# Scatters that alternate with GpSimd's own copies and sums, in a two-block image kernel on one core

## What is computed

```python
x = x + conv0(ln_c(x))        # shared 1x1 conv and 2 of 4 3x3 expert convs an image, group norm, silu
t = to_tokens(x)              # 16 x 1024 tokens of 128 channels
t = t + ffn0(ln_t(t))         # router takes 2 of 8 experts a token: two gated MLP outputs, weighted and summed
x = from_tokens(t)
x = x + conv1(ln_c(x))        # 3x3 depthwise taps made for each image from its pooled channels
t = to_tokens(x)
t = t + ffn1(ln_t(t))         # router takes 1 of 8 experts a token, up to a capacity
x = from_tokens(t)
```

## Time and profile before

| | |
|---|---|
| median of the timed runs | 2088.33 us |
| the profiled execution, its span | 2373.5 us |
| TensorE busy | 1745.3 us, 74% |
| VectorE busy | 1521.7 us, 64% |
| GpSimd busy | 1040.3 us, 44% |
| ScalarE busy | 1020.1 us, 43% |
| GpSimd: scatters L618 | 384, 387.8 us busy |
| GpSimd: scatters L639 | 448, 471.0 us busy |
| GpSimd: sums L670 and L673 | 32, 75.6 us busy |
| granted TensorE clock, mean | 0.879 |

### The profile page before, as it was taken

The page is one execution under the profiler, slowest core; times in us unless marked ns, Lnnn a source line. Parts: engine busy times, 40 slices in busy tenths (PEclk is TensorE's granted clock), DMA queues, the critical chain, the costliest instruction groups (busy, mean ns, idle before and its releaser), DMA issues.

```text
span 2373.5 us, 40208 instructions
## 1 busy us (share of the span) xinstructions
PE 1745.3 (74%) x8924; PEld 941.9 (40%) x8925; DVE 1521.7 (64%) x5423; ACT 1020.1 (43%) x1718; POOL 1040.3 (44%) x1196
## 2 busy tenths in 40 slices
PE   0387777776667775699999999287877868899822
PEld 0333333333333432354445445154544444444312
DVE  1856555545455554577777777476766647788678
ACT  0433333333233332476666667135455524555411
POOL 0003333333333334576566666525455344666600
PEclk9889888878888887799999999599899979999955
DMA  9300001001000002322222221412211013222044
GB/s 267 102 19 28 28 28 36 28 31 33 33 31 28 27 19 59 87 81 74 71 73 79 74 72 46 106 40 60 72 56 45 18 40 95 72 81 72 19 133 151
DMA packets 180085, 149.22 MB, mean 63 GB/s; under 512 B 19302, under 2 KB 161822, under 8 KB 179960
## 3 DMA queue, kind: packets, MB, share of 16 engines
q1 hardware_dynamic: 153336, 98.05, 14.9%
q0 software_dynamic: 26624, 49.93, 6.2%
HBM read 76.00 MB, written 77.34 MB: 65 GB/s over the span
## 4 chain that ended last, share of the span: by engine, by line
PE 38%; DVE 22%; issue 13%; another core or an unknown queue 11%; ACT 7%; POOL 5%; SPq 2%; DMA 1%; ACTq 1%; DVEq 1%; POOLq 0%
PE banks L734 10%; PE banks L736 9%; PE banks L735 9%; PE banks L729 6%; ACT work L1043 3%; POOL slot_rows L618 2%; SPq L429 2%; DVE small L1896 1%; PE banks L747 1%; PE banks L946 1%; DVE small L1392 1%; DVE small L1247 1%; POOL tokens L673 1%; POOL tokens L670 1%
## 5 line engine op out<-in xcount | busy, mean ns | idle before, releaser
L639 POOL DMA_INDIRECT ffn_rows<-work x448 | 471.0, 1051 | 293.9 <-issue 182.1
L618 POOL DMA_INDIRECT slot_rows<-work,small x384 | 387.8, 1010 | 325.5 <-issue 153.3
L729 PE MATMUL banks<-small,work 128*128 128x128 f32 x1472 | 239.9, 308 | 300.8 <-ACT work L1043 118.2
L729 PEld LDWEIGHTS banks<-small,work 128*128 128x128 f32 x1472 | 193.9, 158 | 379.4 <-issue 170.7
L1784 DVE TENSOR_TENSOR work<-work 128x512 f16<-128x512 f32 x376 | 261.4, 695 | 12.8
L734 PE MATMUL banks<-work,wb_h 128*128 128x512 f16 x648 | 247.7, 382 | 26.6 <-DVE work L1800 9.7
L735 PE MATMUL banks<-work,wb_h 128*128 128x512 f16 x648 | 247.0, 381 | 0.0
L736 PE MATMUL banks<-work,wb_l 128*128 128x512 f16 x648 | 246.9, 381 | 0.0
L734 PE MATMUL banks<-work,wa_h 128*128 128x512 f16 x576 | 243.4, 423 | 3.6 <-ACT work L1074 3.3
L735 PE MATMUL banks<-work,wa_h 128*128 128x512 f16 x576 | 243.1, 422 | 0.0
L736 PE MATMUL banks<-work,wa_l 128*128 128x512 f16 x576 | 241.9, 420 | 0.0
(11 more groups left out here) (307 smaller groups left out, 3110.6 us busy)
## 6 DMA issues: line engine op xcount, KB each, us to landing
wa_l<-slot_rows SPq DMA_DIRECT2D x112, 264.0 KB
work<-ffn_rows SPq DMA_DIRECT2D x48, 512.0 KB, 5.2
ffn_rows<-small SPq DMA_DIRECT2D x32, 256.0 KB, 3.7
work<-in_x SPq DMA_DIRECT2D x16, 512.0 KB, 3.3
out_image<-work SPq DMA_DIRECT2D x16, 512.0 KB, 2.6
ffn_rows<-work POOLq DMA_INDIRECT x448
slot_rows<-work,small POOLq DMA_INDIRECT x384
slot_rows<-small SPq DMA_DIRECT2D x17, 264.0 KB, 4.1
```

The costliest lines, as they stand in the source:

```text
L618: pool_e.indirect_dma_start(slots, bass.IndirectOffsetOnAxis(ap=slot_i[:, row_buffer(p, i, k), tt:tt + 1], axis=0), rows[row_buffer(p, i, ...
L639: pool_e.indirect_dma_start(dst, bass.IndirectOffsetOnAxis(ap=idg[old.v][:, qq, 0:1].bitcast(I32), axis=0), yt[old.u][:, qq, :], None, bou ...
L729: last = pe.transpose(dst[:, tt * P:(tt + 1) * P], x, ident)
```

## The change

In stage A ScalarE's copy of rows[0] to rows[1] is gone. GpSimd makes it in 16 pieces of half a block each (64 floats a partition), between its scatters. The new order is S0(0), copies of block 0; then for each further block t: S0(t), half a copy of block t, a wait for the copies of block t-1, S1(t-1), the other half of block t; at the end S1(7). S0 is a scatter of rows[0], S1 one of rows[1]. `A_rows2_ready` now counts 16 pieces an image. `route_rows` waits in addition until the copies of the image before are done, and VectorE's `route_place` waits for the rows themselves and for the scatters of rows[1] of the image before.

In stage C the two sums of an image are cut into eight quarters, each behind one of the eight scatters of a step. They belong to image i+4 instead of i+3 and come after the borders, with the scatters of image i-2, instead of at the start of the step. The first steps, which have no scatters, make the sums whole, in quarters one after another. `C_added` and `C_half_added` count four an image, and those who wait for them are changed to match.

```diff
--- before.py
+++ after.py
@@ -521,7 +521,7 @@
 
             def load_rows(i):
                 if some(i.b - 1):
-                    sp.wait_ge(sem("C_added"), i.b - 1)
+                    sp.wait_ge(sem("C_added"), (i.b - 1) * 4)
                 for k, dst in ((0, ya), (1, yb)):
                     src = back0[bass.ds(i.b * PIX + k * TOKENS, PIX), :]
                     sp.dma_start(dst[i.u], src.rearrange("(t p) c -> p t c", p=P)).then_inc(sem(f"C_rows_loaded{i.u}"), 16)
@@ -602,7 +602,30 @@
             for x in (*pad_h, *pad_l):
                 pool_e.memset(x, 0.0).then_inc(sem("pads_zeroed"), 1)
 
-            def scatters(p, i, choices):
+            def scatter_row(p, i, k, tt):
+
+                pool_e.indirect_dma_start(
+                    slots, bass.IndirectOffsetOnAxis(ap=slot_i[:, row_buffer(p, i, k), tt:tt + 1], axis=0),
+                    rows[row_buffer(p, i, k)][:, tt, :], None, bounds_check=SLOTS - 1, oob_is_err=False
+                ).then_inc(sem(f"{p}scattered_rows{row_buffer(p, i, k)}"), 16)
+
+            def sum_part(i, k, part):
+
+                n = TPI // 4
+                dst = tokens[:, bass.ds(i.b * TPI + part * n, n), :]
+                src = (ya, yb)[k][i.u][:, part * n:(part + 1) * n, :]
+                if k == 0:
+                    if part == 0:
+                        pool_e.wait_ge(sem(f"C_rows_loaded{i.u}"), i.h * 32 + 32)
+                        apart(pool_e)
+                    pool_e.tensor_tensor(dst, dst, src, ALU.add).then_inc(sem("C_half_added"), 1)
+                else:
+                    if part == 0:
+                        pool_e.wait_ge(sem("C_half_added"), i.b * 4 + 4)
+                        apart(pool_e)
+                    pool_e.tensor_tensor(dst, dst, src, ALU.add).then_inc(sem("C_added"), 1)
+
+            def scatters(p, i, choices, more=None):
 
                 if not live(i, IMAGES):
                     return
@@ -613,12 +636,24 @@
                         pool_e.wait_ge(sem(f"{p}scattered_rows{k}"), 16 * TPI * (IMAGES - 2) * choices // 2)
                         apart(pool_e)
                     pool_e.sem_inc(sem("early_rows"), 1)
-                for k in range(choices):
+                if p == "A_":
                     for tt in range(TPI):
-                        pool_e.indirect_dma_start(
-                            slots, bass.IndirectOffsetOnAxis(ap=slot_i[:, row_buffer(p, i, k), tt:tt + 1], axis=0),
-                            rows[row_buffer(p, i, k)][:, tt, :], None, bounds_check=SLOTS - 1, oob_is_err=False
-                        ).then_inc(sem(f"{p}scattered_rows{row_buffer(p, i, k)}"), 16)
+                        scatter_row(p, i, 0, tt)
+                        for half in range(2):
+                            part = slice(half * (C // 2), (half + 1) * (C // 2))
+                            pool_e.tensor_copy(rows[1][:, tt, part], rows[0][:, tt, part]).then_inc(sem("A_rows2_ready"), 1)
+                            if half == 0 and tt:
+                                pool_e.wait_ge(sem("A_rows2_ready"), i.b * (2 * TPI) + 2 * tt)
+                                apart(pool_e)
+                                scatter_row(p, i, 1, tt - 1)
+                    pool_e.wait_ge(sem("A_rows2_ready"), i.b * (2 * TPI) + 2 * TPI)
+                    apart(pool_e)
+                    scatter_row(p, i, 1, TPI - 1)
+                else:
+                    for tt in range(TPI):
+                        scatter_row(p, i, 0, tt)
+                        if live(more, IMAGES):
+                            sum_part(more, tt // 4, tt % 4)
 
             def tile_step(p, i, n, dst, limit):
                 if live(i, n):
@@ -664,21 +699,15 @@
 
 
             def sum_rows(i):
-                dst = tokens[:, bass.ds(i.b * TPI, TPI), :]
-                pool_e.wait_ge(sem(f"C_rows_loaded{i.u}"), i.h * 32 + 32)
-                apart(pool_e)
-                pool_e.tensor_tensor(dst, dst, ya[i.u], ALU.add).then_inc(sem("C_half_added"), 1)
-                pool_e.wait_ge(sem("C_half_added"), i.b + 1)
-                apart(pool_e)
-                pool_e.tensor_tensor(dst, dst, yb[i.u], ALU.add).then_inc(sem("C_added"), 1)
+                for k in range(2):
+                    for part in range(4):
+                        sum_part(i, k, part)
 
             def c_step(i):
                 nxt = i + 1
                 if isinstance(i.b, int) and i.b == -1:
                     for k in range(3):
                         sum_rows(Img(k // 2, k % 2))
-                elif live(i + 3, IMAGES):
-                    sum_rows(i + 3)
                 if live(nxt, IMAGES):
 
                     pool_e.wait_ge(sem("C_low"), nxt.b + 1)
@@ -690,7 +719,9 @@
                     apart(pool_e)
                     pool_e.tensor_copy(v[:, :, :, 0], v[:, :, :, 2]).then_inc(sem("C_border_done"), 1)
                     pool_e.tensor_copy(v[:, :, :, W + 1], v[:, :, :, W - 1]).then_inc(sem("C_border_done"), 1)
-                scatters("C_", i + (-2), 1)
+                if not live(i + (-2), IMAGES) and live(i + 4, IMAGES):
+                    sum_rows(i + 4)
+                scatters("C_", i + (-2), 1, i + 4)
 
             rows_then_tiles(c_step, "D_", TILES1, back1, TOKENS, 4)
 
@@ -1050,6 +1081,8 @@
                 earlier = i.b if p == "A_" else i.h
                 if some(earlier):
                     act.wait_ge(sem(f"{p}scattered_rows{buf}"), earlier * (16 * TPI))
+                    apart(act)
+                    act.wait_ge(sem("A_rows2_ready"), i.b * (2 * TPI))
                 apart(act)
                 tok = lambda tt: tokens[:, bass.ds(i.b * TPI + tt, 1), :].rearrange("p a c -> p (a c)")
                 normalise(p, i, lambda tt: rows[buf][:, tt, 0:C], tok, row_stats, "rows_ready")
@@ -1111,11 +1144,6 @@
                     route_exp("A_", old)
                 if live(nxt, IMAGES):
                     a_silu(nxt, 0)
-                if live(old, IMAGES):
-
-                    if some(old.b):
-                        act.wait_ge(sem("A_scattered_rows1"), old.b * (16 * TPI))
-                    act.activation(rows[1][:, :, 0:C], rows[0][:, :, 0:C], ACT.Copy).then_inc(sem("A_rows2_ready"), 1)
 
             sweep(act, IMAGES, a_step)
 
@@ -1492,7 +1520,11 @@
             def route_place(p, i, choices):
 
 
-                dve.wait_ge(sem(p + ("rows2_ready" if choices == 2 else "rows_ready")), i.b + 1)
+                dve.wait_ge(sem(p + "rows_ready"), i.b + 1)
+                if some(i.b):
+                    apart(dve)
+                    dve.wait_ge(sem("A_scattered_rows1"), i.b * (16 * TPI))
+                apart(dve)
                 bufs = [rows[row_buffer(p, i, k)] for k in range(choices)]
                 for k, buf in enumerate(bufs):
                     dve.tensor_scalar(buf[:, :, C], idf, float(k * TOKENS), None, ALU.add)
@@ -1982,7 +2014,7 @@
                 has_older, has_old, has_nxt, has_far = (live(x, IMAGES) for x in (older, old, nxt, far))
                 seen = 0
                 if isinstance(i.b, int) and i.b == -1:
-                    dve.wait_ge(sem("C_added"), nxt.b + 1)
+                    dve.wait_ge(sem("C_added"), nxt.b * 4 + 4)
                     apart(dve)
                     seen = token_moments(nxt, image_stats)
                     weave(scales(nxt, image_stats, both_eps[:, TPI:2 * TPI], seen))
@@ -1991,7 +2023,7 @@
                 if has_older:
                     choose(older)
                 if has_far:
-                    dve.wait_ge(sem("C_added"), far.b + 1)
+                    dve.wait_ge(sem("C_added"), far.b * 4 + 4)
                     apart(dve)
                     seen = token_moments(far, image_stats)
                 if has_old:
```

## The result

The kernel after takes **2256.01 us** (median of 4 runs, 2254.48 to 2258.98), the kernel before 2088.03 (4 runs, 2085.08 to 2089.49): a ratio of 1.081, 95% interval 1.0793 to 1.0827. That is 168 us slower.

What follows compares the result with a forecast made beforehand. The prediction took the first conv's wait for the single rows[0] buffer as the bound. 2088.3 + 182 (first conv, 15 x 12.1) + 8 (dynamic conv) = 2278 us; range 2140 to 2350.

Steps and rivals of the forecast that it cites:

- The stall: First conv, profiled execution of before: 13 waits of L1100, 132.2 us; timed runs, 285 us shorter, mostly lack it.
- The interval put together from two rows: First conv without the stall: 12.2 us until rows[0] is free plus a 25.8 us chain, 38.0 us an image.
- some 20: Dynamic conv with routing, in timed runs: some 20 us an image, against 25.5 in the trace.
- The scatters of rows[0] already set the pace.: First conv, timed runs before: `route_rows` waits for the previous image's rows[0] scatters, free 12.2 us after the first.
- The order is the cause: First conv: alternating makes rows[0]'s last scatter the 14th instead of the 8th; rows[0] free 12.9 us later.
- The spacing: First conv: scatters with copies between start about 1.65 us apart, bounds 1.28 and 1.87, against 1.28 back to back.
- the first rival: The stall is in timed runs too and hides the late rows[0]: 46 or 98 us, about 2160 us; chance 0.13.
- What TensorE takes back: First conv: TensorE does work ahead of `route_turn` during the wait, taking back at most 0.8 us an image.
- The end of the stage and ScalarE's copy: First conv: last burst 5.6 us longer but covered by SP's tail fills, and removing ScalarE's copy: both about 0.
- The dynamic conv: Quarters of sums between scatters there: +0.6 us for each of 13 images, 8 us, bounds -15 and +35.
- The second: Rival: the stall is real and spaced scatters end it, if spacing is under 1.54 us; 2004 us, chance 0.07.
- The third: Rival: the timed interval doesn't hang on rows[0], scatters being much shorter than traced; about 2088 us, chance 0.03.

Runs made afterwards that it cites:

- run 1: The kernel before, unchanged, profiled a second time: span 2086.8 us, timed 2088.54 us.
- run 3: The kernel before with only the dynamic conv's part of the change: 2098.25 us, ratio 1.0046.
- run 4: The kernel before with GpSimd alternating scatters of rows[0] and rows[1]; ScalarE's copy stays, GpSimd makes none: 2235.51 us, ratio 1.0704.
- run 6: The kernel before with a third row buffer for the first choice of odd images up to 11: 2087.63 us, ratio 0.9999.
- run 9: The dynamic conv's part of the change alone, with two quarters of the sums behind each of scatters 5 to 8: 2080.54 us, ratio 0.9963.
- run 10: The dynamic conv's part of the change alone, with all eight quarters of the sums behind the last scatter: 2081.87 us, ratio 0.9964.
- run 5: The first conv's part of the change alone, but all eight scatters of rows[0], with GpSimd's copies, come before those of rows[1]: 2123.43 us, ratio 1.0182.
- run 7: The kernel after, whole, with a third row buffer for the odd images up to 11: 2132.51 us, ratio 1.0201.
- run 8: The first conv's part of the change alone, plus 36 unused matmuls on TensorE ahead of `route_turn`: 2243.05 us, ratio 1.0748.
- the first conv's half: The kernel before with only the first conv's part of the change: 2248.21 us, ratio 1.0766.

## Why the prediction was right, and where it was not

**The stall** was right, and its cause open. I had inferred from 285 us that timed runs lack it; the second execution shows it. The interval put together from two rows, 38.0 us, is 38.9 in the first twelve, and the dynamic conv's "some 20" is 20.8. What made one execution behave so is not settled: the section of the Trainium skill that I named (NOTIFIC — the notification-queue block, section 7.1) may bear on it, but eleven other profiled executions show no stall, six of them with the same bursts of 16 back to back (runs 1, 3, 4, 6, 9, 10), so recording alone does not bring it about, and no run here shows that block.

**"The scatters of rows[0] already set the pace."** Half right. The wait does end `route_rows` at 12.1 to 12.6 us, but 0 to 1 us behind another that I hadn't looked for, VectorE's row statistics (run 6). The sum survived because it only needs that a later rows[0] is waited for, and not that the present one is.

**The order is the cause.** Right, by runs 4, 5 and 7 together: without copies the loss is there, with copies but in the old order it isn't, and with a third buffer it isn't either. The forecast that the late rows[0] would be the 14th scatter and the last half copy was exact.

**The spacing.** This term was mis-sized: 1.65 us, measured 1.39 (0.98 for the scatter, 0.24 for the copy, 0.17 of start). I read the 1.32 us of the earlier trace rows as a scatter after a copy with the pause of 0.30 inside it. It was the first scatter of a burst. In the first conv such a first one mostly takes 1.72 to 1.79 us and the others 0.97 to 0.99, whether a copy stands between them or not; inside a burst the copy takes the place of the pause. rows[0] came 9.3 us later, not 12.9; that is 54 us too much over 15 hand-overs. The last three intervals of the stage, which were to grow by 12 to 13 us each, are 45.6, 43.9 and 40.8 us in after against 36.0, 34.3 and 31.3 in the second execution of before: 9.5 to 9.6 each. (Two roundings of the working are off by under 1 us: the upper bound of the sum is 28.2 and not 28.3, the first rival's smaller sum 45 and not 46.)

**What TensorE takes back.** Wrong in sign. I subtracted 0.8 us for work ahead of `route_turn`; the way from `route_rows` to the next scatter got 1.0 us longer instead, as TensorE's clock falls in a wait of 10 us (run 8). Over the stage it shows as 0.87 granted in after against 0.96 in before:

```profile
core 0: us, PE busy (x) PEld busy (x) DVE busy (x) ACT busy (x) POOL busy (x), PEclk, DMA share, GB/s
150.00:750.00 600.00, 525.85 (x2766) 271.67 (x2764) 429.51 (x2560) 254.49 (x431) 267.52 (x239) 0.96 0.11 39
```

```profile
core 0: us, PE busy (x) PEld busy (x) DVE busy (x) ACT busy (x) POOL busy (x), PEclk, DMA share, GB/s
150.00:900.00 750.00, 546.34 (x2768) 284.45 (x2765) 439.44 (x2558) 238.82 (x416) 318.75 (x463) 0.87 0.09 31
```

Before (600 us, 525.85 busy) and after (750 us, 546.34 busy) have almost the same matmuls, 2766 and 2768. 9.3 + 1.0 = 10.3 a hand-over, where I had 12.1: 155 us and a few at the stage's start, 160 measured, 182 forecast. The two errors partly cancel, 3.6 us too much for the spacing and 1.8 too little for TensorE, so the first conv's total is nearer than its terms.

**The end of the stage and ScalarE's copy** at nothing: right. From the first scatter of image 15 to the first of the dynamic conv it is 602.8 us with the first conv's half and 602.4 in before.

**The dynamic conv.** The size was near (8 forecast, 10.2 measured), but by luck: the working was not. A quarter is 0.74 us as estimated, a scatter and a quarter 1.92 and not 2.2, and the restart costs nobody anything. In its place stand +17.7 for the diagonals and -7.5 for the rest of the edit to the sums. I had named `tap_weights` as one that a quarter can meet, and put 0.6 us on it all, since I took the block to be as long as the quarter. The trace shows more: around each quarter two diagonals of 0.24 us take 0.8 us each, the first of them still before the quarter starts, so 0.74 us of GpSimd's cost VectorE 1.1. The Trainium skill (SBUF — State Buffer, Who interferes with whom) says that `tensor_scalar` can run in a mode in which it needs the port pair that GpSimd uses, and that one of the two then stands still for a whole instruction. The trace agrees in which instructions suffer: the 128x128 f16 diagonals do, and VectorE's statistics of the tokens (L1918, 1.64 us at 1524.61 with a quarter beside them, 1.64 at 1528.31 without) don't. It does not agree in when: the first of the two slow diagonals starts 0.7 us ahead of the quarter (1514.74 against 1515.44), and why that one is slow stays open. I had cited the same section for another instruction, in which shorter pieces looked like a gain; what decides is which instruction a piece lands beside.

**The rivals.** The first (the stall is real) is out with run 1. The second has half come true: the spacing is under the 1.54 us from which it was to decide, which I had held unlikely; but there was no stall to end. The third is out with runs 4 and 7.

## What to carry to other kernels

When a single buffer is read by a burst, the instruction that matters is the last one that reads it: put it as early in the burst as can be, and count what an interleaving moves behind. A wait that costs nothing to remove may cost in full to lengthen, so ask of each row not only "is it the last" but "how far behind is the next". And before a difference between a profiled execution and the timed runs is explained, take a second profile.

## What was not expected of the hardware

- Scatters back to back stand 1.28 us apart, 0.97 and a pause of 0.30; a copy of 0.24 us between them takes the pause's place, so it costs 0.11 us and not its 0.24 and a start.
- An idle TensorE of 10 us costs 1.2 to 1.6 us more once it resumes (transposes 1.94 for 1.06, matmuls 0.63 for 0.39), with a granted clock of 0.50 for 1.00: 1.2 GHz instead of 2.4. After some 2 us of idleness the transposes took 1.06 to 1.09 us in most images and up to 1.97 in others, in before too (1.97 behind 2.26 us at 252.82, 1.09 behind 2.26 at 410.62).
- A sum of 0.74 us on GpSimd held VectorE's short f16 instructions up for 1.1 us, partly before it began.
- The stall in the first profiled execution, which was 285 us above the timed runs, didn't come back in eleven others.
